# Cross-attention layer on one core: the head of batch 0 reordered, with slot 1's maxima inside the first batch and q ahead of most of K

## The reference, cut to what matters

```python
x = layer_norm(hidden_states, ln1_w, ln1_b)
q = (x @ q_w + q_b).reshape(B, LQ, H, HD).transpose(0, 2, 1, 3)
k = (encoder_hidden_states @ k_w + k_b).reshape(B, LK, H, HD).transpose(0, 2, 1, 3)
v = (encoder_hidden_states @ v_w + v_b).reshape(B, LK, H, HD).transpose(0, 2, 1, 3)
scores = jnp.einsum('bhqd,bhkd->bhqk', q, k) * scale
scores = jnp.where(mask, scores, mask_value)
attn = jax.nn.softmax(scores, axis=-1)
out = jnp.einsum('bhqk,bhkd->bhqd', attn, v)
out = out.transpose(0, 2, 1, 3).reshape(B, LQ, D) @ cproj_w + cproj_b
hidden = out + residual
y = layer_norm(hidden, ln2_w, ln2_b)
y = jax.nn.gelu(y @ fc_w + fc_b, approximate=True) @ proj_w + proj_b
return hidden + y
```

## Time and profile before

| | us |
|---|---|
| median of 3 runs | 765.36 |
| lowest and highest | 765.35, 768.17 |
| the profiled execution | 768.76 |
| its span | 767.0 |

### The profile page before, as it was taken

One profiled execution on the slowest core, in us unless ns is written; L12 is line 12 of the kernel. 1 busy time (PEld: TensorE's weight loads), 2 busy tenths in 40 slices (PEclk: granted clock), 3 DMA queues, 4 the chain that ended last, 5 costly groups with the idle time before them and its releaser, 6 DMA issues.

```text
span 767.0 us, 16866 instructions
## 1 busy us (share of the span) xinstructions
PE 702.5 (92%) x7026; PEld 478.5 (62%) x7026; DVE 371.3 (48%) x824; ACT 446.1 (58%) x475; POOL 120.9 (16%) x90
## 2 busy tenths in 40 slices
PE   3657699899999999999999999999998978999997
PEld 3545466566656656666566566656664544597897
DVE  6643355265436534643464446534642331467663
ACT  3004366856676677567756775676566788733321
POOL 5222002200220032003201220131000600110010
PEclk9867799999999999999999999999999989999999
DMA  9787578657874788477938694878475800000000
GB/s 312 216 186 131 186 184 188 179 138 183 189 203 128 174 188 217 143 180 158 235 123 203 148 246 123 192 153 230 132 165 126 253 6 2 1 21 8 29 28 31
DMA packets 51275, 113.78 MB, mean 148 GB/s; under 512 B 7050, under 2 KB 40178, under 8 KB 49914
## 3 DMA queue, kind: packets, MB, share of 16 engines
q1 hardware_dynamic: 40700, 80.47, 44.5%
q10 hardware_dynamic: 10494, 32.17, 13.8%
HBM read 65.30 MB, written 47.06 MB: 146 GB/s over the span
## 4 chain that ended last, share of the span: by engine, by line
PE 76%; ACT 13%; DMA 5%; DVE 3%; issue 2%; ACTq 1%; DVEq 0%
PE O L1126 21%; PE S L1119 16%; ACT pr L583 11%; PE O L1056 10%; PE XB L1056 10%; PE O L1213 6%; PE S L1056 6%; DMA k_scr<-kpart 2%; DMA qst<-q_scr 2%; PE XB L1093 2%; PE XB L1153 2%; PE MB L1106 2%; DVE kpart L725 1%; DVE kpart L728 1%; DMA cols_s<-in_cols 1%
## 5 line engine op out<-in xcount | busy, mean ns | idle before, releaser
L583 ACT ACTIVATE pr<-S 128x1024 f32<-128x1024 f32 x416 | 400.6, 1024 | 188.6 <-PE S L1119 184.4
L1126 PE MATMUL O<-pr,vsl 128*17 128x256 f32 x3328 | 227.4, 388 | 1.3 <-DVE ot L790 1.3
L1119 PEld LDWEIGHTS S<-qst,kst 50*128 50x128 f32 x1664 | 117.1, 188 | 120.4 <-ACT pr L583 81.4
L1119 PE MATMUL S<-qst,kst 50*128 50x256 f32 x1664 | 171.7, 315 | 18.7 <-ACT pr L583 15.0
L1126 PEld LDWEIGHTS O<-pr,vsl 128*17 128x17 f32 x3328 | 75.3, 97 | 79.2 <-issue 17.7
L725 DVE TENSOR_SCALAR kpart<-O,cols_s 128x384 fp32r<-128x384 f32 x64 | 40.6, 635 | 120.7 <-PE O L1056 120.7
L771 DVE TENSOR_REDUCE mx<-MB 128x2 fp32r<-128x512 f32 x64 | 44.1, 690 | 79.0 <-PE MB L1106 79.0
L510 POOL CAST c_hi<-cT 128x768 fp32r<-128x768 f32 (+1 forms) x28 | 23.9, 852 | 348.0 <-DMA cT<-in_ctx_t 235.8
L1056 PE MATMUL XB<-w_hi,c_hi 128*128 128x256 f32 (+1 forms) x208 | 68.3, 328 | 2.1 <-DVE vsl L739 1.3
L739 DVE TENSOR_TENSOR vsl<-XB,rows_s 128x256 f32<-128x256 f32 (+1 forms) x104 | 43.3, 417 | 55.1 <-PE XB L1056 55.1
L1056 PE MATMUL O<-c_hi,w_hi 128*128 128x384 f32 (+1 forms) x128 | 52.6, 411 | 17.7 <-POOL c_lo L515 10.3
(11 more groups left out here) (100 smaller groups left out, 825.6 us busy)
## 6 DMA issues: line engine op xcount, KB each, us to landing
kst<-k_scr SPq DMA_DIRECT2D x59, 400.2 KB
k_scr<-kpart SPq DMA_DIRECT2D x48, 384.0 KB, 8.0
v_scr<-vsl ACTq DMA_DIRECT2D x8, 1768.0 KB, 11.9
kst<-k_scr SPq DMA_DIRECT2D x59, 200.1 KB
cT<-in_ctx_t ACTq DMA_DIRECT2D x21, 384.0 KB, 7.6
k_scr<-kpart SPq DMA_DIRECT2D x16, 449.0 KB, 7.1
q_scr<-qpart SPq DMA_DIRECT2D x16, 256.0 KB, 2.5
qst<-q_scr SPq DMA_DIRECT2D x59, 64.0 KB
```

The lines of the kernel that those rows point to most:

```text
L583: nc.scalar.activation(pr[:, n % PBUF, :], S[:, 2 * (n % 2):2 * (n % 2) + 2, :] .rearrange("p a n -> p (a n)"), ACT.Exp).then_inc(s_.exp_d ...
L1119: last = nc.tensor.matmul(S[:, 2 * (n % 2) + g_, j * LQ:(j + 1) * LQ], kst[rows_, s, j, kt * P:(kt + 1) * P], qst[rows_, s, j, :], start=T ...
L1126: last = nc.tensor.matmul(O[32 * h:32 * h + VW, 0, 0:LQ], vsl[:, par, s, kt, h * VW:(h + 1) * VW], pr[:, n % PBUF, h * LQ:(h + 1) * LQ], s ...
```

## The change

On TensorE and VectorE, batch 0's q is made after two K units, not four; V units stand behind K units only in K's second half, and V tiles with odd numbers use the bank MB instead of XB. The maxima of slot 1 leave the head and stand at pairs 1 and 2 of batch 0. The wait for the constant rows (ones_in) moves from the fills to TensorE's first maximum. On VectorE the statistics of x, then the mask rows and memsets, then the Newton steps stand ahead of the first K evacuation. SP sends the constant rows first, issues the row "some" behind two K stores, fills one half of slots 0 and 1 and all of slot 2, and loads the rest of x behind the last K store. ACT fills the other half of slots 0 and 1 and loads the context of batch 1 behind that.

```diff
+FIRST_MAX_AT = {1: (0, 1, 0), 2: (0, 1, 1)}
+HEAD_KB = ["k00", "k01", "k02", "k03", "k10", "k11", "k12", "k13", "m00", "m01"]
+HEAD_XB = ["xt", "q", "v0", "v2", "v4", "v6", "v8", "v10", "v12"]
+HEAD_MB = ["v1", "v3", "v5", "v7", "m00", "v9", "m01", "v11"]
...
@@ sync
             load_ctx(sp, 0, 3)
-            sp.dma_start(hid[:, 2 * QT:TOK, :], x[2 * QT:TOK].rearrange("n p d -> p n d")).then_inc(xrest_in, 16)
+            sp.wait_ge(pads_set, 3)
+            constant_rows()
 
             sp.wait_ge(mask_steps, 4)
             sp.dma_start(some_scr.rearrange("o b -> b o"), some_b[:, 1:2]).then_inc(some_out, 16)
             sp.dma_start(mask_scr, mk_f).then_inc(mask_out, 16)
+            store_k(0, 0, 0)
+            store_k(0, 0, 1)
             sp.wait_ge(some_out, 16)
             sp.dma_start(some[:], some_scr[0].partition_broadcast(P)).then_inc(some_in, 16)
-
-            sp.wait_ge(pads_set, 3)
-            constant_rows()
-
-            for c in range(CH):
-                store_k(0, 0, c)
+            store_k(0, 0, 2)
+            store_k(0, 0, 3)
             store_q(0)
             first_fill(sp, 0, 0, [0])
+            first_fill(sp, 0, 1, [0])
             for c in range(CH):
                 store_k(0, 1, c)
+            sp.dma_start(hid[:, 2 * QT:TOK, :], x[2 * QT:TOK].rearrange("n p d -> p n d")).then_inc(xrest_in, 16)
             first_rows(0, 0)
+            first_fill(sp, 0, 2)
             first_rows(0, 1)
@@ scalar
+            first_fill(act, 0, 0, [1])
+            first_fill(act, 0, 1, [1])
             for c in range(CH):
                 next_ctx(1, c)
-            first_fill(act, 0, 0, [1])
-            first_fill(act, 0, 1)
-            first_fill(act, 0, 2)
@@ vector
+            dve.wait_ge(x_in, 16)
+            for n in range(2 * QT):
+                x_stats(n)
+            x_moments(0, 2 * QT, 2 * QT)
             mask_rows()
...
-            dve.wait_ge(x_in, 16)
-            for n in range(2 * QT):
-                x_stats(n)
-            x_moments(0, 2 * QT, 2 * QT)
+            newton(rs_rows(rs1, 0, 2 * QT), ln_steps, XA_VAR, ln_root, 1)
             dve.wait_ge(cols_in, 16)
...
@@ tensor
             k_unit(0, 0, 0)
-            v_unit(0, 0)
             k_unit(0, 0, 1)
-            v_unit(0, 1)
+            xt_unit(0, HEAD_XB.index("xt"))
             k_unit(0, 0, 2)
-            v_unit(0, 2)
+            pe.wait_ge(wqc_in, 16)
+            q_unit(HEAD_XB.index("q"))
             k_unit(0, 0, 3)
...
```

More of the change, by code:

```diff
@@ L93, with max_at @@
 QBLK = LQ // BLK
[L95 to L96 removed]
+FIRST_MAX_AT = {1: (0, 1, 0), 2: (0, 1, 1)}
+HEAD_KB = ["k00", "k01", "k02", "k03", "k10", "k11", "k12", "k13", "m00", "m01"]
+HEAD_XB = ["xt", "q", "v0", "v2", "v4", "v6", "v8", "v10", "v12"]
+HEAD_MB = ["v1", "v3", "v5", "v7", "m00", "v9", "m01", "v11"]
 class Section:
     pass
+def max_at(b):
+    at = {p: w for p, w in MAX_AT.items() if b + w[0] < B}
+    return {**FIRST_MAX_AT, **at} if b == 0 else at
 def kb_pairs(b):
[L105 removed]
+    return sorted((list(K_AT) if b + 1 < B else []) + list(max_at(b)))
 def mb_pairs(b):
[L110 removed]
+    return sorted(max_at(b))
 def xb_pairs(b):
@@ L146 @@
 KB_END = KB_HEAD + sum(len(kb_pairs(b)) for b in range(B))
-HEAD_X = ["v0", "v1", "v2", "xt", "q"] + [f"v{t}" for t in range(3, KT)]
 def k_use(b, mt, c):
-    return HEAD_K.index((mt, c)) if b == 0 else kb_use(b - 1, pair_of(K_AT, (mt, c)))
+    return HEAD_KB.index(f"k{mt}{c}") if b == 0 else kb_use_k(b - 1, pair_of(K_AT, (mt, c)))
 def v_use(b, kt):
-    return HEAD_X.index(f"v{kt}") if b == 0 else xb_use(b - 1, pair_of(V_AT, kt))
-def q_use(b):
-    return HEAD_X.index("q") if b == 0 else xb_use(b - 1, Q_AT)
+    return (HEAD_MB if kt % 2 else HEAD_XB).index(f"v{kt}") if b == 0 else xb_use(b - 1, pair_of(V_AT, kt))
 def rows_use(b, s):
@@ L368, in build, with v_wait @@
         UK = 2 * CH
+        def v_wait(eng, xb, mb, b, kt):
+            eng.wait_ge(mb if b == 0 and kt % 2 else xb, v_use(b, kt) + 1)
         def first_fill(eng, b, s, halves=range(2)):
@@ L532, in _ @@
                     pool.wait_ge(kb_ready, k_use(b - 1, 1, c) + 1)
-                    pool.wait_ge(xb_ready, v_use(b - 1, T0[c] + NT[c] - 1) + 1)
+                    for kt in range(T0[c], T0[c] + NT[c]):
+                        v_wait(pool, xb_ready, mb_ready, b - 1, kt)
                     c_high(b, c)
@@ L1074, in v_unit @@
                 cut = slice((kt - T0[c]) * P, (kt - T0[c]) * P + m)
+                bank, ready, taken = (MB, mb_ready, mb_taken) if b == 0 and kt % 2 else (XB, xb_ready, xb_taken)
                 pe.wait_ge(lo_done, CH * b + c + 1)
-                bank_free(xb_taken, v_use(b, kt))
-                product3(XB[0:m, 0:D], [(c_hi[:, c, k, cut], c_lo[:, c, k, cut]) for k in range(KC)],
-                         [(w_hi[:, 1, k, :], w_lo[:, 1, k, :]) for k in range(KC)]).then_inc(xb_ready, 1)
+                bank_free(taken, v_use(b, kt))
+                product3(bank[0:m, 0:D], [(c_hi[:, c, k, cut], c_lo[:, c, k, cut]) for k in range(KC)],
+                         [(w_hi[:, 1, k, :], w_lo[:, 1, k, :]) for k in range(KC)]).then_inc(ready, 1)
             def xt_unit(b, use):
@@ L1099, in max_unit @@
                 if j == 0:
+                    pe.wait_ge(ones_in, 16 * 6)
                     pe.wait_ge(first.slot_in[s], 16 * FILLS * (b + 1))
@@ L1141, in values @@
                 if n == 0:
-                    pe.wait_ge(xb_taken, v_use(b, KT - 1) + 1)
+                    for t in (KT - 2, KT - 1):
+                        v_wait(pe, xb_taken, mb_taken, b, t)
                 if kt == 0 and SLOTS * b + s > 0:
```

82 lines of the change are left out of this document (36 added, 46 removed).

## The result

The changed kernel is slower. Its median is 783.7 us (781.3 to 784.4, four runs) against 766.4 for the kernel before beside it (four runs): 1.0218 times, 95% interval 1.0186 to 1.025. The prediction was 764.0, range 757.5 to 768.2. The profiled execution took 783.6, its span 781.8, against 768.76 and 767.0: 14.8 us of span to be found.

The account below looks back on a forecast made before the run. A chain through TensorE was taken as the bound, so its start decides: slot 2's maxima at 84.6 against 82.88 lose 1.7 us, 3.1 us of half clock is no longer paid behind them, net 1.4 won: 764.0, range 757.5 to 768.2.

Parts of the forecast that it names:

- The start: Head, q ahead of K: first K evacuation at 17.0, fills start at 33.6, a gain of 0.5 us.
- the bound of 35: Late end for the start of the fills, if the last K store lands after q.
- rival 3: Head doesn't come earlier: fills start at 35, first scores at 71.4, time 765.4; chance 15%.
- The queues: SP and ACT queues, 34 to 61: added loads take 8.8 us, slot 0's rows land behind x, first scores at 70.
- From the first scores to slot 2: TensorE: 11.5 us plus 3.1 for half clock, so slot 2's first maxima at 84.6, without waiting for its fill.
- Slot 3 and the next batch: SP's queue: slot 1's rows and slot 3's fill come later, but are wanted only at pairs 6 and 9; no cost.
- Rival 1: Added loads fit the idle stretch from 54 to 61: scores at 63, 7.5 us won, time 757.9; chance 25%.
- Rival 2: Slower fills and late engines: x lands at 72.6, slot 2 at 88.6; 2.6 us lost, time 768.0; chance 15%.

Follow-up runs that it names:

- slot2_waits_x_again: The changed kernel, with SP waiting for the rest of x to land before issuing slot 2's fill; 773.5 us, 1.0064 times the kernel before.
- after_again: The changed kernel unaltered, run again later beside the kernel before; 779.2 us, 1.0143 times the kernel before.
- slot1_maxima_in_head: The changed kernel with slot 1's maxima moved back ahead of the first scores, behind the last V unit; 774.9 us, 1.0101 times the kernel before.
- both_early: The changed kernel with the rest of x and batch 1's context both loaded early, as before; 766.8 us, 0.9992 times the kernel before.
- maxima_only: The kernel before with only slot 1's maxima moved from the head to pairs 1 and 2 of batch 0; 764.0 us, 0.9969 times.

## Why the prediction was wrong, step by step

**The start.** The sum 9.4 + 6.2 + 1.4 = 17.0 for the first K evacuation was right: 16.93. The subtraction became short as predicted, on VectorE:

```profile
16.93 0.62 DVE L737 TENSOR_SCALAR kpart<-O,cols_s 128x384 fp32r<-128x384 f32 x1
...
27.63 1.00 DVE L768 TENSOR_SCALAR xn<-XB,cols_s,some 128x256 f32<-128x256 f32 x2 [2.00 <-PE XB L1102]
28.66 0.43 DVE L774 CAST qpart<-xn 128x512 fp32r<-128x512 f32 x1
29.12 0.69 DVE L776 TENSOR_TENSOR qpart<-xn,qpart 128x512 fp32r<-128x512 f32 x1
```

0.43 and 0.69 while GpSimd was idle (0.00 us busy from 24 to 35), where the subtraction took 2.17. The fills start at 35.32, 1.2 us later than before, not 0.5 earlier: x landed at 9.79 rather than 9.4 (that the sum came out at 16.93 even so is a little luck), q's product took 3.22 us, over the upper end that I had named, and from q's store to the first fill it took 3.75 us, not 2.92. This is the bound of 35 and rival 3, worth 1.7 us. Over the kernels with this head the fills start between 32.5 and 37.1 (before and its variants 33.9 to 34.9): q ahead of most of K shows no gain beyond that scatter.

**The queues.** This is the step that failed. The place was right: slot 0's rows did land behind x, and TensorE waited, with the V units done at 61.4 (forecast 58.5). The size was not. The sum was 61.1 - 0.5 + 8.8 = 69.4, first scores at 70; they came at 78.41. The term that failed is the 8.8 us for the two added loads: it took them at the 364 GB/s of a free stretch, and only once. The queues did run at 374 GB/s from 54 to 61, but x took 25.0 us from its issue at 51.33 and landed at 76.3, 15.2 us behind the 61.1 at which the last K store had landed before. What the sum left out: the lateness of the few engines was taken as part of the 61.1 and not as a rate at which x itself would be served there; the fill of slot 2 was given to SP right behind the rows and runs against x (5.7 us of the median, by slot2_waits_x_again); and the issue of four small rows took 7.62 us, which held back slot 2's fill but not the rows, as x landed well behind their last issue. My bounds, 63 to 70, both took the loads at full rate; nothing in them let x be slower than any load of the head, though the rows showed a K store of 449 KB that took 18.23 us. Such 18.2 us behind 61.1, as an upper bound, would have been 79.

**From the first scores to slot 2.** Forecast 14.6 us, with no wait for slot 2, 1.5 of it in pair 2 for the bank of the maxima. Measured 14.1 (78.41 to 92.53), no wait for slot 2, and the bank's wait is 1.54. This step was right. The clock cost what was forecast, but not in one piece: 0.63 over 4.6 us and 0.62 over 4.5 make 3.4 us lost, for 3.1.

**Slot 3 and the next batch.** The prediction said that slot 1's rows and slot 3's fill come later "but are wanted only at pairs 6 and 9", and costed that at nothing. Slot 3 was indeed never waited for. But the fill stands on SP's queue ahead of batch 1's stores of K and q, and with the late engines that delays slot 0 of batch 1: a wait of 4.60 us, and 7.2 of lag with the half clock behind it; in after_again the wait is 2.46. So a term put at nothing cost several us. I asked who wants the moved transfer and not who stands behind it. slot1_maxima_in_head takes the wait away, and both_early, with neither load late, still has 2.86 us of it. It would have been missed even with the loads left where they were.

**The rivals.** Rival 1 (the loads fit into the idle stretch) was true of most of the bytes and false of the time. Rival 2 had the right mechanism for the loss, late engines that add up, and put slot 2 at 88.6; it was priced with x landing at 72.6, where it landed at 76.3, and had 15%. The slow side was thus named but both the second place and the size were missing, and 9% for slower was too little.

## What to carry to other kernels

A mean DMA share of 12% with a transfer still out is not free room here: a few engines are late (12% of 16 is two), and whatever spreads over all of them ends when those do. Look first for the transfer with a small slowest dimension; spreading it was worth more here (1.4%) than the order (0.3% in maxima_only). When a transfer moves later on a queue, follow every transfer that then stands behind it into the next batch, not only the engine that reads the moved one. Loads that nobody wants soon were cheapest here ahead of the fills.

## What the runs showed of the hardware that was not expected

- Issuing is not free behind a backlog: with x still out, one issue of 1 KB took 5.96 us on SP (the chain of the changed kernel; those behind it about 0.5), and the rest of x took 4.19, where it took 0.57 early in the kernel before.
- The six products of a K unit took 2.27 us at 18.34 and 1.25 at 95.00, though the rows of the changed kernel show a granted clock of 1.00 at both (18 to 21 below, and 95.0 to 96.3); at 18.34 TensorE had waited before. The record of the clock doesn't explain this; no run isolates it.

```profile
18.00:21.00 3.00, 2.66 (x9) 2.59 (x10) 1.97 (x4) 0.00 (x0) 2.38 (x2) 1.00 0.35 131
```

- A large fill that is issued later makes a small transfer that is already queued land later: 11.89 against 5.55 us. In what order a DMA engine serves them no run isolates.
- The changed kernel gave 1.022 and 1.014 times the kernel before in two groups, with intervals that hardly meet, and its fills started at 35.32 and at 37.10. The traces say where it arises, not why: at slot 3's first maxima the two stand together (111.52 and 111.58), and then the second stall is 4.60 us in one and 2.46 in the other. So figures under some 5 us between groups are not to be relied on.
